# A cross-attention kernel: the third group's Q projection one visit later, the first batch's last K beside its first group, and two loads issued at other times

## The reference, cut to what matters

```python
q = _split_heads(hidden_states @ w_q, HEADS)
k = _split_heads(text @ w_k, HEADS)
v = _split_heads(text @ w_v, HEADS)
out_text = _merge_heads(_sdpa(q, k, v))
k_ip = _split_heads(ip_h @ w_k_ip, HEADS)
v_ip = _split_heads(ip_h @ w_v_ip, HEADS)
out_ip = _merge_heads(_sdpa(q, k_ip, v_ip, mask=mask_ip))
out = (out_text + out_ip) @ w_out + b_out + residual
```

## Time and profile before

| | us |
|---|---|
| median of three runs | 1845.01 |
| lowest and highest of them | 1843.49, 1846.52 |
| the profiled execution, its own time | 1848.91 |
| its span, first to last instruction | 1847.0 |
| PE busy | 1811.4 (98%) |
| DVE busy | 1332.3 (72%) |
| ACT busy | 1185.7 (64%) |

### The profile page before, as it was taken

The page is one execution under the profiler, slowest core; times in us unless marked ns, Lnnn a source line. Parts: engine busy times, 40 slices in busy tenths (PEclk is TensorE's granted clock), DMA queues, the critical chain, the costliest instruction groups (busy, mean ns, idle before and its releaser), DMA issues.

```text
span 1847.0 us, 41069 instructions
## 1 busy us (share of the span) xinstructions
PE 1811.4 (98%) x16856; PEld 718.8 (39%) x16856; DVE 1332.3 (72%) x1787; ACT 1185.7 (64%) x2340; POOL 382.6 (21%) x508
## 2 busy tenths in 40 slices
PE   8999999999999999999999999999999999999988
PEld 3333333433344343433344333343333433434332
DVE  6777777778767787677876777777777777767871
ACT  1276666666666666666666666666666666666766
POOL 5112222211122121122121221112122122221000
PEclk9999999999999999999999999999999999999989
DMA  7555334363344434355453464435544364343410
GB/s 226 102 92 160 67 77 92 73 164 73 74 106 116 106 71 86 94 139 102 79 99 75 141 103 77 97 69 144 94 77 96 72 155 85 74 95 74 77 30 26
DMA packets 103806, 178.16 MB, mean 96 GB/s; under 512 B 42933, under 2 KB 71270, under 8 KB 103618
## 3 DMA queue, kind: packets, MB, share of 16 engines
q1 hardware_dynamic: 82658, 134.12, 37.3%
q0 software_dynamic: 18944, 40.10, 6.9%
q10 hardware_dynamic: 2016, 1.31, 0.2%
HBM read 117.63 MB, written 48.98 MB: 90 GB/s over the span
## 4 chain that ended last, share of the span: by engine, by line
PE 93%; DMA 2%; DVE 2%; SPq 1%; ACT 1%; issue 1%; POOL 0%; ACTq 0%; DVEq 0%; POOLq 0%
PE pv_bank L800 27%; PE max_bank L727 20%; PE work_bank L582 12%; PE exp_bank L784 12%; PE work_bank L604 11%; PE work_bank L627 3%; PE work_bank L593 2%; PE max_bank L745 2%; PE exp_bank L788 1%; DVE tile_max L1069 1%; DMA o_t<-o_sum 1%; SPq L475 1%; ACT probs L978 1%; PE work_bank L658 1%; PE work_bank L611 1%
## 5 line engine op out<-in xcount | busy, mean ns | idle before, releaser
L978 ACT ACTIVATE probs<-exp_bank 128x512 f32<-128x512 f32 x1908 | 1002.0, 599 | 417.3 <-PE exp_bank L784 410.2
L1069 DVE TENSOR_REDUCE tile_max<-max_bank 128x2 f32<-128x1024 f32 x632 | 773.4, 1224 | 400.5 <-PE max_bank L727 395.5
L727 PE MATMUL max_bank<-k_stack,q_stack 48*128 48x512 f32 x1896 | 567.9, 469 | 7.4 <-DVE tile_max L1069 7.3
L800 PE MATMUL pv_bank<-probs,v_ones 128*17 128x512 f32 x3840 | 518.1, 603 | 0.1
L1071 DVE TENSOR_REDUCE tile_max<-max_bank 128x1 f32<-128x512 f32 x632 | 430.2, 681 | 2.7 <-PE max_bank L727 2.7
L784 PE MATMUL exp_bank<-q_stack,k_stack 50*128 50x512 f32 x1908 | 415.9, 403 | 4.0 <-DMA q_stack<-neg_rows 2.7
L727 PEld LDWEIGHTS max_bank<-k_stack,q_stack 48*128 48x128 f32 x1896 | 234.0, 185 | 409.8 <-issue 269.6
L784 PEld LDWEIGHTS exp_bank<-q_stack,k_stack 50*128 50x128 f32 x1908 | 240.0, 188 | 63.2 <-ACT probs L978 47.2
L582 PE MATMUL work_bank<-ctxt,wk 128*32 128x400 f32 x2528 | 253.5, 506 | 7.6 <-DMA wk<-in_w_k 5.5
L604 PE MATMUL work_bank<-wv,ctxt 128*32 128x320 f32 x3040 | 254.0, 435 | 0.0
L604 PEld LDWEIGHTS work_bank<-wv,ctxt 128*32 128x32 f32 x3040 | 93.8, 109 | 163.1 <-issue 100.3
(11 more groups left out here) (124 smaller groups left out, 832.3 us busy)
## 6 DMA issues: line engine op xcount, KB each, us to landing
k_stack<-scratch_k SPq DMA_DIRECT2D x234, 199.2 KB, 6.9
scratch_k<-k_parts SPq DMA_DIRECT2D x80, 400.0 KB, 4.6
ctxt<-in_ctx_t POOLq DMA_DIRECT2D x28, 800.0 KB, 11.1
q_stack<-scratch_q SPq DMA_DIRECT2D x240, 64.0 KB, 2.3
scratch_q<-q_parts SPq DMA_DIRECT2D x80, 128.0 KB, 5.7
r_wide<-scratch_r POOLq DMA_DIRECT2D x39, 256.0 KB, 5.1
xres<-in_x SPq DMA_DIRECT2D x8, 640.0 KB, 9.0
out<-xres SPq DMA_DIRECT2D x32, 160.0 KB, 1.9
```

What stands on the lines that cost most here:

```text
L727: nc.tensor.matmul(round_place(n, r)[:, k, :], exact(q_stack[stack, slot, c, t * 128:(t + 1) * 128]), exact(k_stack[stack, slot, c, chunk ...
L800: last = nc.tensor.matmul(pv_bank[h * 32:h * 32 + VW, :], v_ones[:, v_slot(b, kt), head * VW:(head + 1) * VW], p, start=(kt == 0), stop=(k ...
L978: nc.scalar.activation(dst, exp_place(group_no, at), ACT.Exp, scale=SCALE).then_inc(probs_ready, 1)
L1069: nc.vector.reduce_max(flat[:, at:at + 2], place[:, 0:2, :], AX.X).then_inc(max_taken, 1)
```

## The change

Four edits.

1. **The third group's table (all batches).** Q of the group two ahead moves from visit 0 to visit 1, which has no PV. WA moves from visit 1 to 2, WB from 3 to 4, and the V and K pieces behind them are cut anew.
2. **The last group's K in the first batch.** `("K", 4, 0)` and `("K", 4, 1)` leave group 1 (visits 1 to 5) for group 0 (visits 6 to 10), where later batches have V 9 and V 10. POOL's splits follow (`splits_of`).
3. **The next batch's context in the first batch.** `load_ctx` is issued right behind POOL's split of Q 3, ahead of `spread_recips`, and no longer at the end of g=1. Later batches keep it where it was.
4. **K stacks.** SP waits for `neg_loaded` of the current group before it issues `load_k` of the group two ahead.

```diff
-    if not first:
+    if first:
+        put(0, ("K", 4, 0), 4, (6, 1), (7, 1), (8, 2))
+        put(0, ("K", 4, 1), 4, (9, 3), (10, 1))
+    else:
         put(0, ("V", 9), 4, (6, 1), (7, 1), (8, 2))
         put(0, ("V", 10), 4, (9, 3), (10, 1))
...
-    put(1, ("K", 4, 0), 4, (1, 3), (2, 1))
-    put(1, ("K", 4, 1), 4, (3, 1), (4, 1), (5, 2))
     if not first:
+        put(1, ("K", 4, 0), 4, (1, 3), (2, 1))
+        put(1, ("K", 4, 1), 4, (3, 1), (4, 1), (5, 2))
...
-    put(2, ("Q", 4), 3, (0, 3))
-    put(2, ("WA",), 1, (1, 1))
-    put(2, ("WB",), 1, (3, 1))
+    put(2, ("Q", 4), 3, (1, 3))
+    put(2, ("WA",), 1, (2, 1))
+    put(2, ("WB",), 1, (4, 1))
...
+def splits_of(g, first, last):
+
+    splits = SPLITS[g]
+    if first and g < 2:
+        splits = SPLITS[0] + SPLITS[1][1:] if g == 0 else SPLITS[1][:1]
+    return [p for p in splits if not (last and p[1] > 4)]
...
                         slot_free(group_no + 2)
+
+                        sp.wait_ge(neg_loaded, (group_no + 1) * 32)
                         load_k(group_no + 2)
...
                             split_q(b * NG + piece[1], number(piece))
+                            if first and g == 1:
+                                pool.wait_ge(work_empty, number(("V", FULL)) + 1)
+                                load_ctx(b + 1)
...
-                        if not last:
+                        if not first and not last:
                             load_ctx(b + 1)
```

More of the change, by code:

```diff
@@ L109, in work_plan @@
     if not last:
-        put(2, ("V", 0), 4, (4, 1), (5, 3))
-        put(2, ("K", 5, 0), 4, (6, 1), (7, 1), (8, 2))
-        put(2, ("V", 1), 4, (9, 3), (10, 1))
-        put(2, ("K", 5, 1), 4, (11, 1), (12, 1), (13, 2))
+        put(2, ("V", 0), 4, (5, 3), (6, 1))
+        put(2, ("K", 5, 0), 4, (7, 1), (8, 1), (9, 2))
+        put(2, ("V", 1), 4, (10, 2), (11, 2))
+        put(2, ("K", 5, 1), 4, (12, 1), (13, 3))
         put(2, ("V", 2), 4, (14, 2), (15, 1), (16, 1))
@@ L1330, in body @@
                     group_no = b * NG + g
-                    splits = [p for p in SPLITS[g] if not (last and p[1] > 4)]
+                    splits = splits_of(g, first, last)
                     if group_no + 2 < B * NG:
```

## The result

| | before, us | after, us |
|---|---|---|
| median of 16 runs each, taken side by side | 1841.82 | 1849.07 |
| lowest to highest | 1837.98 to 1846.52 | 1843.19 to 1852.96 |
| ratio after / before, 95% interval | | 1.0031 (1.002 to 1.0043) |
| the profiled execution, its own time | 1848.91 | 1847.33 |
| its span | 1847.0 | 1845.5 |

The changed kernel is slower, by 0.3%: 5.7 us, 3.7 to 7.9 by the interval. (The ratio is that of the means, which are 5.8 us apart; the medians in the table are 7.3 apart.) The two profiled executions say the opposite: the span is 1.5 us shorter after. Where that comes from has to be cleared up before the traces can be compared.

A forecast was written before the change was run, and what follows sets the result against it. PE was taken to bound the kernel, 93% of the chain that ended last. Later batches +2.7 us and the first batch +2.2 made +4.9, put on the median 1845.01: 1849.9 us, range 1842.0 to 1853.5.

The forecast's parts named there:

- the table: Third group, seven later batches: PV 0.26 us earlier, WA adds 0.65, so +0.39 a batch, +2.7 us.
- the queue: First batch, POOL: `scratch_r` lands behind the context, POOL goes on at 157.6, `o_t` lands at 168.0; first batch +2.2 us.
- What bounds the later batches: Start of the third group: the landing of `o_t` ends last, not Q's place; WA's 0.93 us wait is its visible part.
- K 4 into group 0: First batch: group 0 gains 4.55 us, group 1 loses 3.74, net +0.8 us.
- Rival B: First batch: small transfers share the engines, `scratch_r` lands at 151.5, `o_t` at 162.8; 1842.4 us, chance 0.22.
- The wait at the gate: First batch, group 2, before PV of visit 2: PE idle over 4 us until `o_t` has landed, PV at 170.7.
- The charge of 2.3 us for the clock: First batch, group 2, behind PE's idle time: half rate for 6 us, 1.5 of them paced by ACT anyway, 2.3 us.
- The stall on the maxima's transfer: First batch, start of the third group: PE's 2.69 us wait goes, worth some 5.5 us with its slow clock.
- C: Later batches: WA's wait vanishes, -6.5 us, with +2.2 in the first batch 1840.7 us; chance 0.08.
- D: Every batch: longer idle before visit 2 brings the slow clock, 7 x 2 us on top, 1864 us; chance 0.05.
- E: First batch worse than summed, by DVE's inversion before POOL's sums or pack delay reaching the next group: +2 to +4, 1853; chance 0.07.
- A: Whole kernel: the terms as summed, 1849.9 us, own range 1847.5 to 1852; chance 0.58.

The follow-up runs named there:

- after again: The changed kernel, unchanged, profiled a second time; no timed ratio given, its first batch takes 128.3 us.
- after with OUT sooner: The changed kernel with the last OUT piece ending in visit 15 of the second group, nothing else; 0.9975 (0.9959 to 0.9991) against the kernel before.
- OUT sooner: The kernel before with the last OUT piece ending in visit 15 of the second group, not 16; 0.9962 (0.9948 to 0.9976), 7.0 us faster.
- the table alone: The kernel before with only the third group's new table (Q, WA, WB moved); 1.0018 (1.0004 to 1.0033), 3.3 us.
- context behind: The changed kernel with the first batch's context issued behind `scale_o` again, the rest kept; 1.0005 (0.9991 to 1.002) against the kernel before.

## Why the prediction was right

The median came out at 1849.07 against 1849.9. The mechanisms of the two losses, the table and the queue, are those of the prediction. That the first batch's sum came out near its value is in part luck.

**What bounds the later batches: right.** The landing of `o_t` is the gate, Q's place is not. The chain after, and above all the 7.0 us that one moved OUT chunk brings, show it.

**The table, +0.39 a batch: right,** 0.33 by the undisturbed batches. The exponentials moved up to the landing as said, WA stood behind PV as said, and the remaining wait is 0.51 to 0.56 us where some 0.7 was expected. 7 x 0.33 is 2.3 of the 2.7; the timed 3.3 (0.7 to 6.1) doesn't tell them apart. Of the 0.33, 0.27 stand before visit 3 (8.24 against 7.97), so the recut visits behind it lost 0.06 at most.

**K 4 into group 0, +4.55 and -3.74: right in size.** From visit 0 to the tail group 0 takes 43.00 us after (80.12 to 123.12) and 38.67 before: +4.33. Group 1, from its visit 0 to its visit 12, takes 24.36 (124.76 to 149.12) and 27.75: -3.39. The net, +0.9, is the +0.8 of the sum. Timed alone the edit is at 0.9995, where 0.9 us can't be told from none.

**The queue: right.** `scratch_r` behind the context held POOL for 11.87 us, until 156.96, where the sum had 157.6. `r_wide` needed 5.3 us, the product began at 162.22, and `o_t` landed at 167.4 against 168.0. The Trainium skill, page "DMA: Bandwidth & Descriptors", section "Queues, rings and completion order", has descriptors of one ring taken in order; the trace agrees, and the kernel that sends the same transfer from SP's queue agrees as well: 4.6 us. Rival B, whose `o_t` lands at 162.8, is refuted by POOL's wait, although its mechanism has a share: the 9.7 us of `r_wide`.

**The wait at the gate: the size was off.** PE should have been idle for over 4 us, with the slow clock behind it. In the trace of after it is not idle there at all, and slow before it; in the two other traces that show the gate in PE's waits (after again, and after with OUT sooner) it waits 1.85 and 1.96 us. Behind the first of them the granted clock stays up (windows of the second profile of after):

```profile
164.00:168.00 4.00, 2.15 (x29) 0.89 (x27) 2.80 (x3) 1.16 (x3) 0.27 (x1) 1.00 0.57 111
168.00:172.00 4.00, 4.00 (x30) 1.54 (x34) 1.22 (x2) 3.42 (x8) 3.04 (x5) 1.00 1.02 128
```

The charge of 2.3 us for the clock is thus not paid where I put it: the 2.69 us of waiting ahead of the earlier trace rows do not make a rule. Two terms made the wait shorter than forecast: PE came to group 2 later than 160.3 (161.31 there), and `o_t` landed sooner than 168.0 (166.84 there).

**The stall on the maxima's transfer, worth 5.5 us: the step that failed.** It is gone in after, as predicted. But in before it is no constant. Of nine traces with the context in its old place, six have no such wait at all. Two of these six are without edit 4, so the stall can stay away by itself; the other four are all the kernels with edit 4 and a late context, and whether edit 4 keeps it away stays open. The three that have one are before's own (2.69), OUT sooner (0.57) and the table alone, whose line in the waits of PE is

```profile
PE exp_bank L784 <- DMA q_stack<-neg_rows: 1.5, 1, 1.5
```

The transfer takes 7.68 us in before, 6.50 with the table alone and 5.6 with OUT sooner: it stands at the edge, and the profile shown happened to fall on the worst case, 2.9 us above the average of the nine. The forecast credited the change with all 5.5 us of it, though five of the six traces without the wait have a slow stretch all the same. What kept the total right is luck: before's first batch was taken 2.9 us too long, and after's, by the charges for the gate and the slow clock, 1.8 to 2.1 too long (128.2 + 2.2 = 130.4 against 128.6 and 128.3). Against the profile shown the first batch lost 0.5 us (128.6 - 128.2), not 2.2. Against the average of the profiled executions, which is nearer to what the timed runs see, it lost some 3.0. With the table's 2.3 that is 5.3, and 5.7 were timed.

**The sum and the base.** The difference was set on 1845.01, the median of three runs. Over 16 runs before's median is 1841.82, 3.2 lower. So the predicted difference, +4.9, was below the measured one (5.7 by the ratio, 7.3 by the medians), and the base was too high. The two errors have opposite signs, and that the median fell within 0.8 us of the forecast is luck too.

**The other rivals.** C, the wait vanishes: refuted, the chain has `o_t` and the waits moved. D, slow clock in every batch: not seen; of the six batches between the first and the last, one has such a stretch in after (fourth, 47.80 us), and one in before (sixth, 47.62). The last batch has stretches in both kernels. E, the first batch worse than summed by 2 to 4: the loss was 0.8 us above the sum against the average, under E's size, and neither of its mechanisms is seen. Rival B lies inside the stated range, so the range alone would not have told A from B; the rows do.

## What to carry to other kernels

When an engine waits for a small copy, ask what that copy's engine was itself waiting for: moving the copy cost 0.3 us a batch here, and ending one piece of work a visit sooner, three steps up the chain, gave 0.4%. A large transfer issued early on a queue made the small one behind it late by nearly its full length (12.4 us), so what hangs on the small ones belongs in the sum before the large one is moved. And a stall that stands in one profile is worth its average over executions: take a second profile before a forecast is credited with all of it.

## What the runs showed of the hardware that was not expected

The clock falls without a long wait ahead of it. In after, PE was idle for 0.46 us in one piece at 152.5, in a window of which it was busy 3.54 of 4.00, and from about 155 on its granted clock was 0.50 for 13 us. The kernel with the context behind has the same idle piece in the same visit (0.44 us at 151.7), and its clock stays at 1.00. Ten of the fourteen traces have such a stretch that begins between about 152 and 160 us in the same place, some 3 to 13 us long, with the early context and with the late one, with K moved and without. The kernel with the context behind and the one with OUT sooner alone have none there; before's own and the table alone have one only behind their wait for the maxima. A short one is that of the second profile of after (windows):

```profile
155.00:158.00 3.00, 3.00 (x14) 1.02 (x6) 1.49 (x6) 0.48 (x2) 0.71 (x1) 0.59 0.09 14
158.00:162.00 4.00, 4.00 (x28) 1.42 (x27) 3.11 (x5) 2.34 (x5) 0.40 (x1) 1.00 0.15 61
```

What sets its length, and whether it falls at all, stays open: no run here changed it on purpose. It is the largest source of scatter in the first batch with a late context (122.9 to 126.6 us, by the table and its text), and in the last batch the sum of two distances of the same work differs by 5.4 us (79.45 and 74.01) with 17 and 3 us at the lower level.

The 8 KB transfer `scratch_r` was waited for 2.08 us with nothing large ahead; from issue to the next step it took 4.6 us on another queue beside 3.2 MB, and 12.4 on the same queue behind them. A 256 KB one (`r_wide`) took 5.2 us before, with the context not yet issued, and 9.7 beside it.
